# Freeing the buffers of gathered rows in groups of four instead of sixteen

## What is computed

```python
def _L3_ffn_ref(x, Wq_pk, pk_keys, Wq, keys_table, values_table, Wo):
    # DIM 64, HEADS 8, NUM_KEYS 64, PK_TOPK 16, FINAL_TOPK 16
    q = (x @ Wq).reshape(b, n, HEADS, DIM) * DIM ** (-0.5)
    kv_scores, indices = _pk(x, Wq_pk, pk_keys)      # 16 weights and 16 table rows per token and head
    ind = indices + offsets[None, None, :, None]
    k = jnp.einsum('bnhk,bnhkd->bnhd', kv_scores, keys_table[ind])
    v = jnp.einsum('bnhk,bnhkd->bnhd', kv_scores, values_table[ind])
    ...                                              # causal softmax attention of q over k, v
    return out.transpose(0, 2, 1, 3).reshape(b, n, HEADS * DIM) @ Wo
```

## Time and profile before

| | us |
|---|---|
| median of 3 runs | 16746.29 |
| lowest and highest run | 16664.32 to 16760.74 |
| profiled execution, first to last instruction | 16598.0 |
| stretch of the last stage that holds the copies of gathered rows | 5452 to 16404 |

### The profile page before, as it was taken

One profiled execution on the slowest core, in us unless ns is written; L12 is line 12 of the kernel. 1 busy time (PEld: TensorE's weight loads), 2 busy tenths in 40 slices (PEclk: granted clock), 3 DMA queues, 4 the chain that ended last, 5 costly groups with the idle time before them and its releaser, 6 DMA issues.

```text
span 16598.0 us, 138013 instructions
## 1 busy us (share of the span) xinstructions
PE 10426.9 (63%) x38094; PEld 5354.4 (32%) x38094; DVE 8776.5 (53%) x22927; ACT 6776.6 (41%) x14111; POOL 6839.7 (41%) x5848
## 2 busy tenths in 40 slices
PE   1656756646663566666666666666666666666667
PEld 1322222223131233333333333343333333333334
DVE  3538979974856444444444444444444444444441
ACT  0225434421021444544444444444444444444443
POOL 3007757750000544444444444444444444444441
PEclk9757878876775677887777777787777777778776
DMA  0003323320000111111111111111111111111110
GB/s 21 12 3 120 123 90 123 122 77 14 10 7 18 39 39 37 40 38 36 39 39 37 35 40 36 40 37 40 38 35 40 36 41 34 40 37 39 38 36 18
DMA packets 538604, 723.53 MB, mean 44 GB/s; under 512 B 412866, under 2 KB 420593, under 8 KB 503386
## 3 DMA queue, kind: packets, MB, share of 16 engines
q0 software_dynamic: 168448, 338.54, 7.8%
q1 hardware_dynamic: 369418, 376.55, 7.3%
HBM read 697.87 MB, written 8.42 MB: 43 GB/s over the span
## 4 chain that ended last, share of the span: by engine, by line
PE 26%; another core or an unknown queue 19%; ACT 11%; issue 7%; DVE 3%; DVEq 1%; ACTq 0%
PE l3m_acc L2569 6%; PE l3m_O L2540 5%; ACT l3m_spread L2665 4%; PE l3m_S L2523 3%; PE l3m_DX L2559 3%; PE l3m_T L2530 3%; ACT l3m_prob L2694 2%; PE l3m_S L2559 2%; ACT l3m_V L2707 2%; ACT l3m_W L2711 2%; ACT l3m_probT L2703 1%; PE l3m_T L2483 1%; PE l3m_DX L2560 1%; PE l3m_T L2508 1%
## 5 line engine op out<-in xcount | busy, mean ns | idle before, releaser
L2465 POOL DMA_INDIRECT l3m_got<-in_l_table,l3m_row x5120 | 4928.0, 963 | 6110.9 <-ACT l3m_spread L2665 3560.0
L2569 PE MATMUL l3m_acc<-l3m_W,l3m_values 128*128 128x512 f32 x3072 | 2038.9, 751 | 1302.8 <-issue 656.5
L2947 DVE SCALAR_TENSOR_TENSOR tower_h<-l3m_O,l3m_pinv,tower_h 128x64 f32<-128x64 f32 x512 | 145.3, 284 | 3392.4 <-PE l3m_O L2540 2470.2
L2665 ACT ACTIVATE l3m_spread<-l3m_got,l3m_weight 128x128 f32<-128x128 f32 x5120 | 1926.8, 495 | 24.2 <-DVE l3m_kv L2927 12.7
L2703 ACT ACTIVATE l3m_probT<-l3m_T 128x512 f32<-128x512 f32 (+3 forms) x1280 | 684.9, 535 | 2173.6 <-remote 1446.2
L2540 PE MATMUL l3m_O<-l3m_vo_g,l3m_probT 128*128 128x64 f32 x5440 | 864.9, 306 | 901.8 <-ACT l3m_probT L2703 668.2
L1325 POOL TENSOR_TENSOR m_mul<-m_st,m_wide_c 128x2048 f32<-128x2048 f32 x256 | 1158.4, 4525 | 432.3 <-DVE m_st L1598 426.6
L2540 PEld LDWEIGHTS l3m_O<-l3m_vo_g,l3m_probT 128*128 128x128 f32 x5440 | 822.1, 221 | 1161.7 <-ACT l3m_probT L2703 811.1
L2569 PEld LDWEIGHTS l3m_acc<-l3m_W,l3m_values 128*128 128x128 f32 x3072 | 599.5, 225 | 1662.4 <-issue 837.6
L2530 PE MATMUL l3m_T<-tower_ident,l3m_prob 128*128 128x128 f32 x4352 | 846.5, 318 | 400.0 <-issue 242.7
L2711 ACT ACTIVATE l3m_W<-l3m_DX 128x512 f32<-128x512 f32 x971 | 578.0, 595 | 1125.8 <-remote 681.1
(11 more groups left out here) (694 smaller groups left out, 20714.0 us busy)
## 6 DMA issues: line engine op xcount, KB each, us to landing
m_wide_c<-l1a_c SPq DMA_DIRECT2D x256, 1024.0 KB, 4.6
l3m_got<-in_l_table,l3m_row POOLq DMA_INDIRECT x5120
l3m_values<-in_l_table SPq DMA_DIRECT2D x288, 256.0 KB
l0i_img<-in_l_x SPq DMA_DIRECT2D x4, 1024.0 KB, 8.1
l2r_x<-l2a_hT SPq DMA_DIRECT2D x8, 512.0 KB, 5.4
qp_inw<-in_q_inw SPq DMA_DIRECT2D x1, 2336.0 KB, 7.8
l_kept<-l0t_xt,l0t_row POOLq DMA_INDIRECT x128
l1a_c<-m_listf SPq DMA_DIRECT2D x16, 128.0 KB, 4.9
```

The source lines that it names most:

```text
L2465: pool.indirect_dma_start(got[:, unit % GOT, j, :], None, table, bass.IndirectOffsetOnAxis(ap=row[:, unit // QUAD % RING, unit % QUAD, j:j ...
L2569: pe.matmul(acc[:], values[:, tile, :], W[:], start=(tile == 0), stop=(tile == TILES - 1)).then_inc(blended, 1)
L2665: copy = act.activation(spread[:, unit % 2, :, j], got[:, unit % GOT, j, :], ACT.Copy, scale=weight[:, g % RING, t, j:j + 1])
```

## The change

`parted` counts groups of four copies. ACT increments it after every fourth copy of a unit, not only after the sixteenth (1,280 increments in place of 320). POOL waits in front of rows 0, 4, 8 and 12 of a unit for the matching group of the unit four back, not once in front of row 0 for all sixteen. DVE's wait is for the same copy as before, told in the new count. The number of buffers, the rows, the copies and their order stay.

```diff
-GOT, RING = 4, 5
+GOT, RING, FREED = 4, 5, 4
...
+        def copies_done(unit, rows):
+            return (unit * TOPK + rows) // FREED
...
                 if unit % QUAD == 0:
                     pool.wait_ge(found, unit // QUAD + 1)
-                if unit >= GOT:
-                    pool.wait_ge(parted, unit - GOT + 1)
                 for j in range(TOPK):
+                    if unit >= GOT and j % FREED == 0:
+                        pool.wait_ge(parted, copies_done(unit - GOT, j + FREED))
                     pool.indirect_dma_start(got[:, unit % GOT, j, :], None, table,
...
-                    if j == TOPK - 1:
+                    if j % FREED == FREED - 1:
                         copy.then_inc(parted, 1)
...
-                dve.wait_ge(parted, unit + 1)
+                dve.wait_ge(parted, copies_done(unit, TOPK))
```

## The result

The change made the kernel faster: 15,371.9 us against 16,753.5, a ratio of 0.918 (95% interval 0.915 to 0.921), 1,382 us. The profiled spans differ by 1,236 us. The forecast was 15,750, in a range of 14,800 to 16,650.

The account below looks back on a forecast made before the run. POOL's 16-row runs, holding up the other engines, were taken as the bound. Shorter runs save 1,220 us, late units lose 220: 16,598 - 1,000 = 15,598, plus 148 for the median, 15,750 us; range 14,800 to 16,650.

Parts of the forecast that it names:

- The bound: Copies' stretch: POOL's 16-row runs hold up the hand-over between engines, 10.2 us a unit, 3,260 us over 320 units.
- quiet steps: Check of the bound: two steps with no row issued took 14.6 us each, 6.8 below the mean, so 3,480 us.
- the yardstick: PE's busy time lost in and after a run, 9.4 us, divided by 0.926 to give 10.2 us of step list.
- Edits costed at nothing: Earlier issue, 960 more ACT increments and 960 added POOL waits: all three 0; increments 58 us at the far end.
- Shorter runs: POOL's rows go in runs of 8, 8 and 4 per 20, with pauses between; saves 6.5 us per unit.
- two ends: Pauses between POOL's runs: 1.5 us or more is enough to start afresh, or it isn't (the slower rival, 0.08).
- Where it doesn't apply: Units whose row numbers come late from DVE still go out in long runs: 132 units, 220 us lost.
- late quads: The 33 times POOL waits for DVE's row numbers, 1,075 us, counted as 132 units not helped.
- The sum: (320 - 132) x 6.5 = 1,220 us, less 220, makes 1,000 us saved from the profiled span.
- Signs to look for: POOL idle behind ACT's copy 700 times or more, PE's unexplained idle time down a third, clock above 0.79.
- The page's rule: SBUF: transfers and engines use separate ports, PE and ACT never wait; gives the nothing-moves rival's result, 16,750 us, chance 0.12.

Follow-up runs that it names:

- m2: Kernel before with another rule per quarter: 1.1-us pauses, groups of eight, only 4 of 16 rows (quarter 3), SP issuing plain rows; 14,077.4 us against 16,808.0.
- h1: Changed kernel with each group of four rows freed 32 copies later; 14,567.6 us against 16,742.1 for the kernel before, ratio 0.869.

## Why the prediction was right, and where it was off

*The bound.* Right: the stage was bound by what POOL's long runs do to the others, not by an engine's work. But I priced it too low. I said 3,260 us, and 3,480 by the quiet steps. The chips without the hold-up run the kernel before 4,190 us faster (16,750 against 12,560), and quarter 3 of m2 says nearly the same, (2,771 - 1,764) x 4 = 4,030. The weak step is the yardstick, lost busy time at whatever clock. In the 5 us that begin 2 us after a run of 16 rows PE is busy 3.65 us, which I took as nearly whole, but over the 269 such stretches of the kernel before the granted clock is 0.57, against 0.96 in the first 5 us of the same runs. My quiet steps, 14.6 us each, were not quite undisturbed either: an undisturbed step is 1,764 / 128 = 13.8 us.

*Edits costed at nothing.* Right: no wait for rows (14 us), and copies at 495 ns.

*Shorter runs.* The mechanism is right, self-limiting included: POOL stops soon after it stops ACT. I expected runs of 8, 8 and 4 rows, and runs of 4 were the most (312 of 570). That 1.5 us of pause is enough was the value I chose between two ends, and the trace of after gives 4.56 of 5 us for 1.5 to 2 us. Runs of 8 lose a little more than I took (3.22, not 3.49).

*Where it doesn't apply.* I assumed 33 late quads and 132 units without a gain. There were 63 waits for row numbers, but fewer of their rows stayed in long runs: those in runs of 4 to 12 are 312 x 4 + 83 x 8 + 90 x 12 = 2,992 of 5,120, 58%, and I had 188 of 320 units, 59%.

*The sum.* 1,000 us forecast, 1,236 between the profiled spans. The terms can be measured: cut both traces at the start of each run of rows, and take as the loss of a piece its time less 1,763.5 / 1,280 = 1.378 us for each copy that starts in it (the undisturbed pace of quarter 3 of m2, so this is an estimate). The kernel before loses 3,985 us, 12.45 a unit; I had 10.2. In the changed kernel the runs of 4 to 12 rows (187 units) lose 6.2 a unit, where I had 4.6 x 16 / 20 = 3.7. The two prices were too low by about the same, so that their difference, 6.2, nearly equals the 6.5 of the sum: that is partly luck. The mis-sized term is the one for late units. I had 132 units that lose 1.7 us more than before, 220 us. The runs of over 16 rows (108 units) lose 13.3 us a unit, 0.9 more, 90 us, and another 25 units, in runs of 16, gain 5.7 each. So 187 x 6.2 + 25 x 5.7 - 90 = 1,210 us. These 60 long runs make up 1,435 of the 2,764 us that the changed kernel still loses, and the later groups of h1 win by doing away with them.

The other part of the miss, 15,372 against 15,750, isn't in the kernel: I added 148 us because the profiled execution of the kernel before was that much below its median, and for the changed kernel the two are 10 us apart. Hence 1,382 us between the medians and 1,236 between the spans.

*Signs to look for.* POOL's stops behind ACT were to be 700 or more and were 500. PE's idle time with no visible cause ("issue" in the waits view, over the copies' stretch) was to fall by a third and fell from 1,625 to 1,287 us, 21%. The clock rose above 0.79, as said.

*The page's rule.* The Trainium skill's "SBUF — State Buffer", section "SBUF: two separate sides", would have PE and ACT untouched. Chips 8, 13 and 15 agree with it: the kernel before takes 12,560 us there. Chips 4, 5 and 7 disagree as to the effect (16,530 to 16,810 us). That rows written by SP's DMAs disturb nobody there (1,727 us a quarter) agrees with the rule; that the rows issued by POOL do, it doesn't foresee. Whether a port has part in it no run here shows.

*What stays open.* Why chips differ. Three had the hold-up and three didn't, with the same kernel; the chip of the first result isn't on record. Only chip 4 came twice, with the hold-up both times, so that it belongs to the chip and not to the hour isn't shown. Which part of POOL's work it is: with SP both the issuer and the form (plain, fixed rows) changed, and the run that should have parted them fell on a chip without the effect. And what is held up: the traces show late starts and late ends of waits, not the resource. The changed kernel itself wasn't run on a chip without the hold-up; two variants of it were, and were equal to the kernel before.

## What to carry to other kernels

When no engine is busy and none waits for a visible partner, line up the windows of many like stretches by the start of some other engine's run: a stall that depends on the time since a start is a mechanism, and here it hung on runs of indirect DMAs issued from GpSimd. Let the consumer release such DMAs in small groups, and as late as its data allow rather than as early as they could. And put the control into the kernel, quarter against quarter: three of the six chips didn't have the effect at all, and a comparison across runs would have mixed the two.

## What the hardware showed unexpectedly

The same kernel takes 12,560 us on some chips and 16,530 to 16,810 on others. The runs of one set agree within 0.8%; chip 4 gave 16,536 us in one set and 16,808 in another, so chips with the effect are less steady than those without, where all lies between 12,529 and 12,587. The whole difference is in this stage, and within 1% it vanishes with 4 rows in a run (1,764 us a quarter), with 2.26-us pauses behind every fourth row (2,083, its floor), or with SP as the issuer of plain rows (1,727). On a chip with the effect it sets in about 5 us, four rows, into a run. Behind a run of four it is over after some 1.5 us; behind one of 16 PE is busy only 0.47 of the first 2 us. On a chip without it, 6,400 us of rows nearly in one piece do nothing.
